# Where the block of maxima stands in a step: ahead of the step's other products, or behind them

## The reference

```python
x = x + 0.5 * ffn(layernorm(x), W, b)      # W is rounded to -s, 0, s; one 512x512 product
x = x + attn(layernorm(x), Wqkv, bqkv, Wo, bo)
x = x + 0.5 * ffn(layernorm(x), W, b)

def attn(x, ...):                          # 16 heads of 32
    kqv = x @ Wqkv + bqkv
    scores = einsum('bsnh,btnh->bnst', k, q) / sqrt(32)   # s: keys of the softmax's rows, t: the other side
    scores = triu(scores) - 10000 below the diagonal
    attn = softmax(scores, axis=2)
    return einsum('bnkq,bknh->bqnh', attn, v) @ Wo + bo
```

## Time and profile before

| | |
|---|---|
| median of 3 runs | 1210.66 us (1209.63 to 1210.69) |
| the profiled execution's own time | 1212.57 us |
| its span, first to last instruction | 1210.8 us |
| TensorE busy | 1143.3 us, 94% of the span |
| ScalarE busy | 946.1 us, 78% |
| VectorE busy | 750.1 us, 62% |
| GpSimd busy | 347.0 us, 29% |
| mean granted TensorE clock | 0.952 of full speed |

### The profile page before, as it was taken

How to read it: one execution, slowest core, us unless ns; L and a number is a source line. 1 busy time by engine, 2 the same in 40 slices (tenths; PEclk the granted TensorE clock), 3 DMA queues, 4 the chain that set the end, 5 groups by cost and what they waited for, 6 DMA issues and landing times.

```text
span 1210.8 us, 26364 instructions
## 1 busy us (share of the span) xinstructions
PE 1143.3 (94%) x9466; PEld 718.4 (59%) x9466; DVE 750.1 (62%) x2304; ACT 946.1 (78%) x2699; POOL 347.0 (29%) x503
## 2 busy tenths in 40 slices
PE   4688999899999999999999999999999999998996
PEld 3465556465666666665666666665666666654555
DVE  6865434479844666779745666779744666654344
ACT  1248887888888888888888888888888888888541
POOL 4821120035401232335401232335301332301243
PEclk9898978789999999999999999999999999997599
DMA  7431311011112211231112211330112212100121
GB/s 252 150 102 54 106 44 48 29 54 54 38 45 71 72 38 54 83 122 54 46 38 71 72 37 61 115 104 33 46 37 71 72 37 72 37 3 2 37 68 38
DMA packets 41969, 77.72 MB, mean 64 GB/s; under 512 B 5488, under 2 KB 11632, under 8 KB 41840
## 3 DMA queue, kind: packets, MB, share of 16 engines
q1 hardware_dynamic: 41840, 76.04, 18.8%
HBM read 49.81 MB, written 25.17 MB: 62 GB/s over the span
## 4 chain that ended last, share of the span: by engine, by line
PE 76%; DVE 10%; ACT 8%; issue 2%; POOL 2%; DMA 1%; SPq 0%; DVEq 0%; ACTq 0%; POOLq 0%
PE bank L1047 27%; PE bank L1107 14%; PE bank L1137 11%; PE bank L1159 10%; PE bank L1072 7%; ACT masked_scores L953 5%; DVE masked_scores L800 4%; PE bank L1064 3%; PE bank L1143 3%; DVE st L749 1%; DVE hn L768 1%; ACT prob L981 1%; DVE qT L776 1%; DVE xt L788 1%; ACT qT L904 1%
## 5 line engine op out<-in xcount | busy, mean ns | idle before, releaser
L800 DVE CUSTOM_DVE_ANT_0 masked_scores<-bank,mask 128x512 f32<-128x512 f32 (+3 forms) x768 | 382.1, 554 | 297.9 <-PE bank L1107 263.2
L953 ACT ACTIVATE masked_scores<-masked_scores,mst 128x512 f32<-128x512 f32 (+3 forms) x768 | 463.7, 610 | 48.1 <-DVE mst L800 47.5
L981 ACT ACTIVATE prob<-bank 128x512 f32<-128x512 f32 (+3 forms) x768 | 311.9, 491 | 40.2 <-PE bank L1143 39.2
L1107 PE MATMUL bank<-kT,qT 32*128 32x512 f32 (+2 forms) x2304 | 203.6, 404 | 14.9 <-ACT prob L981 8.4
L701 POOL TENSOR_SCALAR_AFFINE_SELECT prob<-prob 128x512 f32<-128x512 f32 x128 | 81.5, 637 | 448.5 <-ACT prob L981 447.5
L1107 PEld LDWEIGHTS bank<-kT,qT 32*128 32x128 f32 x2304 | 115.1, 191 | 159.3 <-issue 71.9
L1047 PE MATMUL bank<-hT,wqk 128*128 128x512 f32 x768 | 197.4, 407 | 0.0
L1137 PE MATMUL bank<-qT,kT 32*128 32x512 f32 (+2 forms) x2304 | 185.9, 394 | 5.2 <-DVE mst L800 4.5
L1047 PEld LDWEIGHTS bank<-hT,wqk 128*128 128x128 f32 x768 | 143.2, 193 | 37.6 <-ACT prob L981 7.1
L1137 PEld LDWEIGHTS bank<-qT,kT 32*128 32x128 f32 x2304 | 105.8, 192 | 83.5 <-issue 57.2
L1159 PE MATMUL bank<-prob,v 128*32 128x512 f32 (+3 forms) x1344 | 149.4, 518 | 0.0
(11 more groups left out here) (87 smaller groups left out, 1008.8 us busy)
## 6 DMA issues: line engine op xcount, KB each, us to landing
wqk<-weight_scratch SPq DMA_DIRECT2D x30, 512.0 KB, 3.3
wvo<-weight_scratch SPq DMA_DIRECT2D x20, 512.0 KB, 6.0
xt<-in_L_attn_x_dram SPq DMA_DIRECT2D x32, 256.0 KB, 3.6
residual_scratch<-xt SPq DMA_DIRECT2D x32, 256.0 KB, 2.0
xt<-residual_scratch SPq DMA_DIRECT2D x32, 256.0 KB, 2.8
out_dram<-xt SPq DMA_DIRECT2D x32, 256.0 KB, 2.0
o<-in_L_attn_Wqkv_dram SPq DMA_DIRECT2D x12, 256.0 KB, 4.7
weight_scratch<-o SPq DMA_DIRECT2D x6, 512.0 KB, 2.9
```

The source lines that it names most:

```text
L800: nc.vector.tensor_tensor_reduce(masked_scores[:, h, 0:n], psum(u, h)[:, 0:n], mask[:, off:off + n], -SCALE, BIG, ALU.add, ALU.min, mst[:, ...
L953: nc.scalar.activation(of, of, ACT.Exp, bias=mst[:, c + kc, at:at + 1], scale=-1.0, accum_out=ssum[:, c + kc, at:at + 1]).then_inc(a_free, 1)
L981: nc.scalar.activation(prob[:, at % 2, h, off:CW], psum(("S", b, n), h)[:, off:CW], ACT.Exp, scale=SCALE)\
L1107: m = nc.tensor.matmul(psum(u, h)[:, 0:n], query_piece(b, g, c)[row, x, P * r:P * r + P], kT[g % 2][row, y, CW * kc:CW * kc + n], start=(t ...
```

## The change

In a slot that has a step, `uses()` now gives the whole uses first and the block of maxima last. TensorE's, VectorE's and ScalarE's streams follow it: TensorE computes scores, values, M/N/C/T, the large product, the block of maxima, and then the next step's scores. VectorE takes the four maxima after its operations on the step's other products. ScalarE takes the four sums of the block after the high half of a P or the copy of a V; before, three of the four stood ahead of it. The ring's banks are dealt out in the new order. Head and tail keep theirs.

```diff
@@ -195,7 +195,7 @@
     def uses(self):
-        return self.blocks + self.whole
+        return self.blocks + self.whole if self.step is None else self.whole + self.blocks
@@ -262,7 +262,7 @@
 for s in SLOTS:
-    small = [u not in PRODUCTS for u in s.uses()]
+    small = [u not in PRODUCTS for u in s.whole]
     assert small == sorted(small, reverse=True)
@@ -873,7 +873,7 @@                                   # VectorE
                 for u in s.uses():
-                    if u not in PRODUCTS:
+                    if u not in PRODUCTS and (u[0] != "A" or s.step is None):
                         use(u)
@@ -881,6 +881,8 @@
                 for u in s.uses():
                     if u in PRODUCTS:
                         use(u)
+                for u in s.blocks if s.step is not None else []:
+                    use(u)
@@ -999,15 +1001,15 @@                                # ScalarE
-                for u in s.blocks:
-                    block_sums(u, range(4) if u != s.blocks[-1] else range(3))
+                for u in s.blocks if s.step is None else []:
+                    block_sums(u, range(4))
                 for u in s.uses():
                     if u[0] == "P":
                         high(u)
                     elif u[0] == "V":
                         keep_values(u)
-                if s.blocks:
-                    block_sums(s.blocks[-1], (3,))
+                for u in s.blocks if s.step is not None else []:
+                    block_sums(u, range(4))
```

## The result

The changed kernel takes 1452.65 us (median of four runs, 1450.89 to 1455.34) against 1210.68 us: slower by a factor of 1.199, with a 95% interval of 1.194 to 1.203. The profiled execution has a span of 1451.4 us, 240.6 more than before.

The account below looks back on a forecast made before the run. TensorE, busy 94% of the span, was taken as the bound. Terms 109 + 36 + 36 - 10 = 171 us, plus 50 for the clock, gave 221 on 1212.57: forecast 1430 us, range 1345 to 1500.

Parts of the forecast that it names:

- The scores wait for the maximum just ahead: TensorE's fourth score product waits for the bank of the first head's maxima: 0.6 us in 182 steps, 109 us.
- Steps with an F, O or V have no addition: In the 71 steps without P or T, the block's own 0.9 us covers the residual: nothing added.
- P steps: 60 steps: VectorE's low half of P precedes the first maximum, 0.6 us more each, 36 us beyond the bank wait.
- T steps: 51 steps with T and no P: a two-engine loop outlasts TensorE's step, 0.7 us each, 36 us beyond the bank wait.
- the loop over ScalarE: In T steps, ScalarE and VectorE work between first maxima takes 7.3 us against TensorE's 6.6: 36 us in all.
- N and M count for nothing of their own: N and M waits, now ahead of the block that covered them, were counted inside the loop's price.
- 10 us of waits go: The block of maxima no longer follows the scores, so most of its 8.4 us waiting for exponentials goes: 10 us off.
- The clock: More TensorE time at the lower clock level, 1.2 GHz, from waits in every step: 50 us, between 0 and some 200.
- The row of 80 to 380 us at 0.90: Stretch of the earlier trace, partly steps with only A, clock 0.90 against 0.95 overall; basis of the 50 us.
- The loop without the clock: Rival: all three added terms and no additional low clock, 1382 us (1350 to 1395); chance 0.19.
- only the bank wait: Rival: ScalarE's high halves stay hidden and the clock holds, 1310 us, 1345 with half the P and T terms; chance 0.12.
- not slower: Rival: the first maximum is read out before the fourth score product, all 12.9 us of waits go, 1198 us; chance 0.03.

Follow-up runs that it names:

- the shorter maximum: First head's maximum taken over 64 columns only, in both orders: 1394.69 us on the changed kernel, 1199.82 us on the kernel before.
- only_p: The kernel before with the new order only in the 60 steps whose row has a P: 1348.34 us.
- the fillers: The changed kernel with two full products of constant data ahead of each step's scores: 1416.31 us; the kernel before with three at 25 places: 1201.88 us.
- the three runs: The kernel before with the new order only in P steps, only in T steps without P, or only in the other 71: 1348.34, 1329.38, 1286.42 us.

## Why the prediction was right

The forecast was 1430 us in 1345 to 1500; 1452.65 was measured. By its steps:

- **The scores wait for the maximum just ahead (109 us).** Right as a mechanism. The timeline has the wait, and the shorter maximum moves the new order by 58 us and the old by 10. The term was 0.6 us for each of 182 steps. In the 22 steps with no large product the old order has that wait already, as the prediction's own show, so their 13 us should not have been counted: behind these steps the scores' idle wait for a maximum is 4.7 us before and 5.6 us after. The 49 steps with an F, O or V had 29 us from this term and lost 39.
- **Steps with an F, O or V have no addition.** Not quite. The residual was to be covered by the block of maxima; behind these steps the scores wait 4.2 us for one, ten times, and did not before. Together with the term above the errors nearly cancel: 43 us were given for the 71 steps and 37 measured (39 and -2). That the sum fits so well is in part luck.
- **P steps (0.6 + 0.6 a step, 72 us).** Right: 77 us without the clock, in the changed kernel and again in only_p. The maximum starts 1.49 us after the block, 1.6 was given.
- **T steps (0.6 + 0.7 a step, 67 us).** The sum was near, 56 us. The part for the loop over ScalarE was too large: undoing ScalarE's order gave 15 us of it, where 36 stood. The loop's larger effect was on the clock, 65 us at the low level in these steps and 10 without the loop. What is left, 41 us without the clock, is more than the 31 us of the bank wait: 11.0 us of the scores' idle time there is for the residual of F or O, which VectorE takes ahead of the first maximum.
- **N and M count for nothing of their own.** Mis-sized. N's and M's waits together are 19.6 us and were 3.7 us. They lie in the kinds' sums above, so the terms that carried them were a little large for what they named.
- **10 us of waits go.** The idle wait for exponentials fell from 8.4 to 5.6 us only. But the whole of the maxima's group, busy and idle, is 31 us shorter, so the idle times alone understate what went. How much of the 31 was waiting that counts as busy was not separated.
- **The clock (50 us).** Right in kind and too small: 0.952 to 0.913 is up to 68 us. The row of 80 to 380 us at 0.90 that it was taken from was not a bad guide in size: from 100 to 1410 us the changed kernel has 0.91. This term is most of the 20 us by which the forecast was short: without it 171 us were given and about 173 came. Two slips in the sums change nothing: 1212.57 and 221 make 1434 rounded, and in the T step's time on TensorE the 2.05 is 2.14 by the rows (620.14 to 622.28).
- **The rivals.** The loop without the clock (1382 us) is out by the clock of 0.913 and by the fillers, which made the kernel faster; only the bank wait (to 1345 us) by the P and T steps; not slower by the first maximum, which lets the fourth product of the scores start 1.1 us late in the P step shown and 0.7 us late in the step with N, T and F (653.72 to 655.50, against 1.1).

Of the signs that the prediction named, most came: TensorE busy 88%, the clock at 0.913, 1.49 us to the first maximum, and steps with a T longer than those with only a V (7.56 against 6.56 us on the mean). One did not come as written. The scores' idle waits sum to 92.9 us and not to 100 or more; 87 waits, not some 170, are put down to the maximum, and 70, not some 100, to low halves (60 of P, 10 of T). The idle time of TensorE leaves out what is waited behind an issued product: the scores' busy time rose by 122 us with the same products.

Of the Trainium skill's two statements that stood in the prediction ("TensorE: Matmul & The Clock Gate"), the one on PSUM cycling ("A second HAM failure mode: psum-queue depth-cycling") agrees with the trace in what it says would be seen: with many brief waits, of at most 0.9 us in front of the scores, the clock goes between its two levels, with 136 us more at the lower one. That the brief waits are the cause no run here shows, as said at the fillers. The advice of the same page against long idle gaps ("Why this matters for your kernels") is not enough here: between 280 and 1290 us TensorE's longest wait is 1.9 us, and the clock fell 24 times. (The kernel before has waits of up to 3.0 us that the earlier trace rows leave out, for a normalised tile, but they lie outside 90 to 1150 us, and its clock fell within that stretch too.)

The expectation that failed was that of additivity. The price of P and T steps in the new order is the same alone and together, that of the F, O and V steps is 28 us alone and 39 together; what comes on top is paid where the orders change, 46, 50 and 34 us in the old-order steps of the three runs.

## What to carry to other kernels

Count how many banks lie between two uses that both take several of them: with 4 and 4 from a ring of 7, one next to the other, there is always one bank that the second takes from the first, and how much other work stands between the two decides whether that bank is free in time. Put the long product there, but look at what else the move shifts: in the run with small uses, maxima and then the product, other waits and some clock cost 77 us. Where a wait of half a microsecond comes in each of 182 steps, it costs its sum, and here the clock fell with it. And an operation in an in-order stream is as late as what stands ahead of it: look at what it stands behind on each engine, not only at what it needs.

## What was not expected of the hardware

Extra matmuls made both orders faster. 364 full products of 128x512 took 36 us off the changed kernel (clock 0.913 to 0.957), and 75 took 8 us off the kernel before (0.952 to 0.983). And the clock is not told by TensorE's idle time: it fell in the kernel before at the end of a stretch recorded as wholly busy, and a kernel with a third less of the scores' idle time kept nearly the same clock (0.918 against 0.913).
